# Four graph layers on one core: places of the adds computed ahead of their waits, layer 1's scores and one-hots in another form, and the last layer's adds dealt out between linked operations

## The chip, the cores and the metric

One NeuronCore of a Trainium2 chip runs the whole kernel as a single program. The metric is the device time of one execution in microseconds (us); less is better.

## The reference

`x` holds 3125 nodes of 256 features; 53125 edges (25000 in both directions and 3125 loops), sorted by target, join them. Four layers follow each other. Each normalises `x`, adds a sum over the edges and a linear attention over all nodes ("mix"), and then a feed-forward part of eight experts. What matters here is the sum over the edges:

```
layer 0:  x += elu-like( sum over edges of weight * (xn @ W)[src] ) + mix0(xn)
layer 1:  score[e,h] = sum over d of q[dst,h,d] * (k[src,h,d] + relation[type,d])
          alpha = softmax of score over the edges of one target
          x += f( sum over edges of alpha * v[src] ) + mix1(xn)
layer 2:  like layer 1 with logits  leaky_relu(s[src] + t[dst]), 8 heads
layer 3:  x += relu( segment_sum( (xn @ W)[src] * edge_weight, dst ) )
             + x-mixing: K,Q = elu+1; KV = K^T V; out = Q KV / (Q sum K);
               layer_norm(out @ Wm); relu([x, out] @ W1) @ W2; layer_norm
```

## The kernel before, in words

The edges are packed into 440 **steps** of 128 edges each. All targets of a step lie in one tile of 125 nodes, and a register holds the tile's number. In every layer a step goes through the same stations: the rows of its 128 sources are fetched (GpSimd issues an indirect DMA in layers 0, 2 and 3 and in the scores of layer 1; in layer 1's sums SyncE loads rows that were kept in order), a **one-hot** matrix (edge by node of the tile) is made on VectorE by comparing a ramp 0..124 with each edge's local target, TensorE multiplies one-hot by rows into a PSUM bank (the pages show it as two MATMULs per step), and VectorE's **add** puts the bank onto the rows of `total` that belong to the step's tile. The next step may go to the same tile, so every add waits for the one ahead of it (semaphore `added`) as well as for its own product (`summed`). TensorE may run ahead of the adds by as many banks as there are: 7 in layers 0 and 1, 3 in layers 2 and 3. The place of the add in `total` depends on the tile's register, so VectorE's queue computes an address by a register operation. It stands in the order lists as `ISA` and in the trace as `DVEq FUSED_REGOPS`.

Nothing schedules this at run time: each engine's instructions stand in the order in which the Python functions emit them, and semaphores tie the engines together.

- **Layer 0**, `Sums` (`gathered_sums`): per step one one-hot with its weight (`match`, eight steps ahead, L854) and one add (L880).
- **Layer 1, scores**, `edge_scores`: two steps form a **pair**. In a **turn** VectorE adds the relation (L3249), multiplies with the query the pair of the turn before (L3253), and sums over the 64 features of each head the pair of two turns before (L3257) if its number is even; odd pairs are summed on ScalarE, by eight activations with an accumulator (L3171). Only then are the pair's 2 of 12 row slots free for the next fetch of 256 KB. Layer 1's mixing (`MemoryMix`: `pe_turn`, `act_turn`, `dve_turn`) is cut into turns as well and rides along; ScalarE's share of a turn stands behind the scores of that turn.
- **Layer 1, sums**, `weighted_sums`: GpSimd multiplies the rows with alpha (L3438), the one-hots are made for eight steps at a time (`compare`, L3458), the add is L3466, and 24 slots hold rows.
- **Layer 2**, `Attend`: adds in L3977, each eighth in L3979, amid ten other operations on VectorE.
- **Layer 3**, `WeighedSums` in `gnn3_mix3`: one-hots for eight steps (L919), weights on ScalarE (L912), adds in L943. The mixing stands in **slots** (`kv`, `context`, then for thirteen node runs `q`, `read0`, `read1`, `out`, `turn`, `hidden`, `y`). A slot has steps in proportion to its work: 11 in `hidden`, 5 or 6 in `y`, 3 in `out`, 1 or 2 in the reads. TensorE does a slot's mixing first and then its steps. VectorE does the slot's adds first and then its mixing, except in `read0` and `read1`. Much of that mixing is a chain of small operations, each waiting for the one before (`link`).

Of the kernel before, what the change touches and what calls it, by code (L numbers as in the profile page):

```python
# [8 lines left out]
ALU = mybir.AluOpType  # L9
# [6 lines left out]
D = 256  # L16
P = 125
# [41 lines left out]
class Chain:  # L59
# [16 lines left out]
    def link(self, ins):  # L76
        self(ins)
        self.settle()

# [732 lines left out]
class Sums:  # L812
# [69 lines left out]

class WeighedSums(Sums):
# [48 lines left out]
    def add(self, v, s):  # L932
# [6 lines left out]
        tile = self.tiles.at(s)  # L939
        v.wait_ge(self.summed, s + 1)  # L940
        v.wait_ge(self.added, s)
        there = self.total[:, bass.ds(tile, 1), :]
# [1676 lines left out]
def gnn3_mix3(core):  # L2619
# [10 lines left out]
    with Phase(nc, "g3") as outer:  # L2630
        gnn3_front(core, table)
        total = outer.sb("total", [P, NT, D])
        with Phase(nc, "m3") as ph:
# [149 lines left out]
            def _(v):  # L2783
                link = Chain(v, mixing.chain_sem).link
# [28 lines left out]
                v.wait_ge(mixing.loaded, mixing.nload)  # L2813
                for (stage, r, _), steps in zip(slots, spans):
                    if stage not in ("read0", "read1"):
                        for s in steps:
                            sums.add(v, s)
# [6 lines left out]
                    elif stage == "read0":  # L2824
                        mixing.read_dve(v, link, r, 0)
                        for s in steps:
                            sums.add(v, s)
                        if r >= 2:
                            normalise(r - 2)
                    elif stage == "read1":  # L2830
                        mixing.read_dve(v, link, r, 1)
                        for s in steps:
                            sums.add(v, s)
# [8 lines left out]
                    elif stage == "y":  # L2842
# [14 lines left out]
class MemoryMix:  # L2857
# [107 lines left out]
    def act_turn(self, act, turn):  # L2965
        nc, H = self.core.nc, self.H
        if turn == self.LENGTHS + NODE_LOOPS - 1:
            act.wait_ge(self.summed, 1)
            nc.scalar.activation(self.root[:], self.total[:], ACT.Sqrt).then_inc(self.rooted, 1)
        if turn == self.SHIFT + 9:  # L2970
            act.wait_ge(self.kshift, 1)
            nc.scalar.activation(self.memk[:], self.memk[:], ACT.Exp).then_inc(self.mem_grown, 1)
        t = turn - self.CONTEXT
        if 0 <= t < NT:
# [5 lines left out]
        o, j = divmod(turn - self.READ, self.PERIOD)  # L2980
        if 1 <= o <= NODE_LOOPS and j == 0:
            act.wait_ge(self.summed2, o)
            nc.scalar.activation(self.root2[:], self.total2[:], ACT.Sqrt).then_inc(self.rooted2, 1)
        if 0 <= o < NODE_LOOPS:
            if j == BODY + 3:
                act.wait_ge(self.qshift, o + 1)
                nc.scalar.activation(self.q, self.q, ACT.Exp).then_inc(self.qgrown, 1)
            k, stage = divmod(j - 12, 2)
            if 0 <= k < BODY:
                t = o * BODY + k  # L2990
                if stage == 0:
                    act.wait_ge(self.turned, t + 1)
                    if t >= 2:
                        act.wait_ge(self.read, t - 1)
                    nc.scalar.activation(self.qT[:, t % 2, :], self.banks[t % 2][:, 0:P], ACT.Copy).then_inc(self.qkept, 1)
                else:
                    act.wait_ge(self.read, t + 1)
                    if t >= 2:
                        act.wait_ge(self.result, t - 1)
                    nc.scalar.activation(self.outT[:, t % 2, :], self.banks[t % 2][:, 128:128 + P], ACT.Copy).then_inc(self.okept, 1)  # L3000
# [104 lines left out]
def edge_scores(core, name, table, kept, query, relation, factor, scores, heads):  # L3105
# [11 lines left out]

    def pair_on_act(pair):
        return pair % 2 == 1

    def pairs_of_act(pair):
        return sum(pair_on_act(p) for p in range(pair + 1))

    with Phase(nc, name) as ph:
# [8 lines left out]
        expanded, shifted, multiplied, scored, act_scored = (ph.sem(n) for n in ("expanded", "shifted", "multiplied", "scored", "act_scored"))  # L3133
# [42 lines left out]
        @block.gpsimd  # L3176
        def _(pool):
            for s in range(STEPS):
                k = s % SLOTS
                if s >= SLOTS:  # L3180
                    pair = (s - SLOTS) // 2
                    if pair_on_act(pair):
                        pool.wait_ge(act_scored, pairs_of_act(pair))
                    else:
                        pool.wait_ge(scored, pair + 1 - pairs_of_act(pair))
# [30 lines left out]
        def _(v):  # L3216
# [24 lines left out]
            for turn in range(PAIRS + 2):  # L3241
# [12 lines left out]
                if 2 <= turn and not pair_on_act(turn - 2):  # L3254
# [5 lines left out]
            v.wait_ge(scored, PAIRS - pairs_of_act(PAIRS - 1))  # L3260
            v.wait_ge(act_scored, pairs_of_act(PAIRS - 1))
# [130 lines left out]
def weighted_sums(core, name, source, alpha, heads, total, own, values):  # L3392
# [5 lines left out]
    SLOTS, BANKS = 24, 7  # L3398
    PAIRS = STEPS // 2
    dim = D // heads  # L3400
    with Phase(nc, name) as ph:
        rows = ph.sb("rows", [W, SLOTS, D + heads])
        same = ph.sb("same", [W, 3, GROUP, P])
# [37 lines left out]
        def _(pe):  # L3441
            for s in range(STEPS):
# [3 lines left out]
                if s % GROUP == 0:  # L3446
                    pe.wait_ge(same_set, s // GROUP + 1)
                if s >= BANKS:
                    pe.wait_ge(added, s - BANKS + 1)
                nc.tensor.matmul(banks[s % BANKS][0:P, 0:D + heads], same[:, s // GROUP % 3, s % GROUP, :], rows[:, s % SLOTS, :], start=True, stop=True).then_inc(summed, 1)  # L3450

        @block.vector
        def _(v):
            def compare(g):
                shape = [W, GROUP, P]
                if g >= 3:
                    v.wait_ge(summed, GROUP * (g - 2))
                nc.vector.tensor_tensor(same[:, g % 3], bcast_mid(ramp[:, 0:P], shape), bcast_last(core.local[:, g * GROUP:(g + 1) * GROUP], shape),  # L3458
                                        ALU.is_equal).then_inc(same_set, 1)

            def add(s):
                tile = tiles.at(s)
                v.wait_ge(summed, s + 1)
                v.wait_ge(added, s)
                there = total[:, bass.ds(tile, 1), :]
# [8 lines left out]
            compare(0)  # L3474
            compare(1)
# [301 lines left out]
class Attend:  # L3777
# [190 lines left out]
    def add(self, v, s):  # L3968
# [3 lines left out]
        v.wait_ge(self.summed, s + 1)  # L3972
        if s:
            v.wait_ge(self.added, s)
        there, bank = self.total[:, bass.ds(tile, 1), :], self.banks[s % self.BANKS][0:P, 0:D + self.heads].unsqueeze(1)
# [338 lines left out]
```

## Time and profile before

| | |
|---|---|
| times of 3 runs | 6445.46, 6431.71, 6440.05 us |
| median | 6440.05 us |
| the profiled execution's own time | 6485.74 us |
| its span, first to last instruction | 6484.0 us |
| TensorE busy | 4404.0 us (68%) |
| VectorE busy | 3177.3 us (49%) |
| ScalarE busy | 1424.5 us (22%) |
| GpSimd busy | 2731.1 us (42%) |
| mean granted TensorE clock | 0.799 of full speed |

The kernel is a row of phases with barriers between them, so the shares of the whole say little: each phase has an engine, a queue or a chain of its own that sets its length. Line numbers are those of the kernel before.

### The profile page before, as it was taken

To read this page: it belongs to the slowest core of one execution; us is meant where nothing else is said; L and a number is where in the kernel's file an instruction comes from. 1 tells how busy PE (TensorE), PEld (TensorE's weight loads), DVE (VectorE), ACT (ScalarE), POOL (GpSimd) and SP (SyncE) were. 2 spreads that over 40 slices of the span, in tenths; PEclk is the share of its full clock that TensorE was granted. 3 is DMA by queue.
4 is the path that set the end of the run, shared out by engine and by line. 5 is a ranking of instruction groups with operands and counts; after the bars stand their busy time and mean duration, and the time that the engine had idled before them with its cause. 6 is when DMAs were issued, how large, how long until landed. Compare 5 with 4: busy or idle time off the path is not lost. (4 is left out here: it accounts for less than half of the span.)

```text
span 6484.0 us, 70548 instructions
## 1 busy us (share of the span) xinstructions
PE 4404.0 (68%) x18134; PEld 3067.0 (47%) x18134; DVE 3177.3 (49%) x7287; ACT 1424.5 (22%) x4712; POOL 2731.1 (42%) x2772
## 2 busy tenths in 40 slices
PE   0398855556795666664883946878759996788743
PEld 0256533334583343332342834666537774566543
DVE  7235444443004556666773135788842224577622
ACT  0022200002222233331132311100023333333211
POOL 1456656661101545553663035666400005566332
PEclk9988866667898575556995977887779998899776
DMA  4100023333012778884633224433310003222323
GB/s 150 53 2 2 2 66 92 92 91 88 34 35 85 235 231 236 241 235 143 187 94 107 72 70 106 106 102 103 69 40 0 0 2 100 77 87 88 77 97 107
DMA packets 407853, 616.81 MB, mean 95 GB/s; under 512 B 76553, under 2 KB 304286, under 8 KB 407109
## 3 DMA queue, kind: packets, MB, share of 16 engines
q0 software_dynamic: 124448, 324.61, 18.3%
q1 hardware_dynamic: 279908, 284.99, 13.9%
q10 hardware_dynamic: 3154, 3.20, 0.2%
q8 instruction: 147, 2.41, 0.2%
q14 instruction: 196, 1.60, 0.1%
HBM read 475.70 MB, written 137.50 MB: 95 GB/s over the span
## 5 line engine op out<-in xcount | busy, mean ns | idle before, releaser
L838 POOL DMA_INDIRECT m_rows<-support,far_at x440 | 444.3, 1010 | 989.9 <-POOLq L97 746.5
L3187 POOL DMA_INDIRECT g_sc_rows<-keyval,src_at x440 | 431.6, 981 | 492.7 <-DVE g1b_scores L3257 275.5
L3813 POOL DMA_INDIRECT g_sp_rows<-h,src_at x440 | 456.3, 1037 | 276.5 <-PE g_sp_bank L3862 142.8
L848 PE MATMUL g_sums_bank<-g_sums_rows,g_sums_same 128*125 128x256 f32 x880 | 351.8, 539 | 294.7 <-issue 277.4
L493 POOL DMA_INDIRECT records<-record,place_at x416 | 419.0, 1007 | 282.5 <-issue 121.0
L838 POOL DMA_INDIRECT g_sums_rows<-h,far_at x440 | 415.9, 945 | 232.2 <-issue 116.0
L3206 PE MATMUL g_sc_pair<-g1q_parts,g_sc_near 125*128 x1320 | 330.1, 381 | 151.6 <-DVE g_sc_rows L3253 100.5
L848 PEld LDWEIGHTS g_sums_bank<-g_sums_rows,g_sums_same 128*125 128x125 f32 x880 | 200.9, 257 | 445.6 <-issue 398.3
L3862 PE MATMUL g_sp_bank<-g_sp_rows,g_sp_same 128*125 128x264 f32 x880 | 315.1, 467 | 117.3 <-DVE g_total L3977 61.6
L880 DVE TENSOR_TENSOR g_total<-g_total,g_sums_bank 125x256 f32 x440 | 182.7, 415 | 336.2 <-issue 150.0
L906 PE MATMUL m_half<-m_rows,m_marks 128*125 128x256 f32 x880 | 268.8, 425 | 106.2 <-issue 76.4
L3171 ACT ACTIVATE g_sc_rows<-g_sc_rows 128x64 f32<-128x64 f32 x880 | 211.9, 242 | 518.7 <-DVE g_sc_rows L3253 415.6
L3450 PE MATMUL g_sp_bank<-g_sp_rows,g_sp_same 128*125 128x260 f32 x880 | 280.9, 427 | 53.9 <-DVE g_total L3466 36.3
L943 DVE TENSOR_TENSOR g_total<-g_total,m_half 125x256 f32 x440 | 184.6, 420 | 241.8 <-PE m_half L906 109.7
L3438 POOL TENSOR_TENSOR g_sp_rows<-g_sp_rows,g_alpha 128x512 f32<-128x512 f32 x220 | 226.7, 1042 | 173.4 <-DMA g_sp_rows<-kept 171.9
L3249 DVE TENSOR_TENSOR g_sc_rows<-g_sc_rows,g_sc_pair 128x512 f32<-128x512 f32 x220 | 150.2, 683 | 285.1 <-DMA f_back<-answer_rows,f_place_at 120.0
L1378 DVE SCALAR_TENSOR_TENSOR x<-f_y,f_comb,x 125x256 f32 x200 | 96.7, 483 | 376.4 <-PE f_y L1195 376.4
L1672 POOL DMA_INDIRECT f_back<-answer_rows,f_place_at x100 | 95.1, 951 | 411.4 <-DMA answer_rows<-f_answer 381.6
L1237 ACT ACTIVATE f_hid<-f_h,f_shift,f_scale 128x375 f32<-128x375 f32 (+1 forms) x320 | 195.4, 611 | 286.4 <-PE f_h L1174 280.6
L906 PEld LDWEIGHTS m_half<-m_rows,m_marks 128*125 128x125 f32 x880 | 160.6, 202 | 191.8 <-issue 119.8
L3862 PEld LDWEIGHTS g_sp_bank<-g_sp_rows,g_sp_same 128*125 128x125 f32 x880 | 165.1, 216 | 178.5 <-issue 101.8
L3206 PEld LDWEIGHTS g_sc_pair<-g1q_parts,g_sc_near 125*128 125x128 bf16 x1320 | 137.3, 119 | 217.5 <-issue 169.2
(702 smaller groups left out, 9995.7 us busy)
## 6 DMA issues: line engine op xcount, KB each, us to landing
kept<-g_sc_rows SPq DMA_DIRECT2D x440, 128.0 KB
g_sp_rows<-kept SPq DMA_DIRECT2D x440, 128.0 KB
xnT<-sorted_rows SPq DMA_DIRECT2D x80, 256.0 KB
answer_rows<-f_answer SPq DMA_DIRECT2D x64, 256.0 KB
g_sc_local_in<-local_rows SPq DMA_DIRECT2D x55, 250.0 KB
g_sp_local_in<-local_rows SPq DMA_DIRECT2D x55, 250.0 KB
answer_rows<-zero SPq DMA_DIRECT2D x1, 9856.0 KB
sorted_rows<-zero SPq DMA_DIRECT2D x1, 8192.0 KB
```

The source lines that it names most:

```text
L493: nc.gpsimd.indirect_dma_start(core.records, bass.IndirectOffsetOnAxis(ap=core.place_at[:, t:t + 1], axis=0), core.record[:, t, :], None). ...
L838: nc.gpsimd.indirect_dma_start(self.rows[:, k, :], None, self.table, bass.IndirectOffsetOnAxis(ap=core.far_at[:, s:s + 1], axis=0)).then_i ...
L848: nc.tensor.matmul(self.halves[s % slots], self.same[:, s % self.RING, :], self.rows[:, s % self.SLOTS, :], start=True, stop=True).then_in ...
L906: nc.tensor.matmul(self.halves[s % slots], self.mark(s), self.rows[:, s % self.SLOTS, :], start=True, stop=True).then_inc(self.summed, 1)
L1237: nc.scalar.activation(hid[layer][:, i % 2, mo, 0:n], hbank[q % HR][:, 0:n], func, scale=scale[layer][:, g, mo:mo + 1], bias=shift[layer][ ...
L3171: ins = nc.scalar.activation(product, product, ACT.Copy, accum_out=scores[:, h, s:s + 1])
L3187: nc.gpsimd.indirect_dma_start(rows[:, k, :], None, table, bass.IndirectOffsetOnAxis(ap=core.src_at[:, s:s + 1], axis=0)).then_inc(gathere ...
L3206: nc.tensor.matmul(banks[pair % PAIR_BANKS][:, s % 2, 0:D], near[:, g % 2, k * W:(k + 1) * W], query[:, i, bass.ds(tile, 1), :].rearrange( ...
L3438: nc.gpsimd.tensor_tensor(mine, mine, alpha[:, 2 * pair:2 * pair + 2, :].unsqueeze(3).to_broadcast([W, 2, heads, dim]), ALU.mult).then_inc ...
L3450: nc.tensor.matmul(banks[s % BANKS][0:P, 0:D + heads], same[:, s // GROUP % 3, s % GROUP, :], rows[:, s % SLOTS, :], start=True, stop=True ...
L3813: nc.gpsimd.indirect_dma_start(self.rows[:, k, :], None, self.table, bass.IndirectOffsetOnAxis(ap=core.src_at[:, s:s + 1], axis=0)).then_i ...
L3862: nc.tensor.matmul(self.banks[s % self.BANKS][0:P, 0:D + self.heads], self.same[:, g % 2, k, :], self.rows[:, s % self.SLOTS, :], start=Tr ...
```

## The change

Four edits, in the words of the code:

1. Every `add` (four classes or functions) lowers its place (`v.lower_ap(there)`), that is emits the register operation, ahead of its two waits, and waits for `added` before `summed`.
2. `edge_scores`: all pairs are summed on VectorE; ScalarE's program is layer 1's mixing alone, written out in order (`act_program`).
3. `weighted_sums`: a one-hot is made per step, eight steps ahead, in a ring of 16, in place of one instruction for eight steps.
4. `gnn3_mix3`: `Woven` holds back up to a number of a slot's adds (`links`) and emits one behind each linked operation of the slot's mixing; what is left follows at its end.

```diff
+class Woven(Chain):
+    def __init__(self, eng, sem, fill):
+        Chain.__init__(self, eng, sem)
+        self.fill, self.left = fill, []
+    def open(self, steps, ahead):
+        self.left = list(steps)
+        while len(self.left) > ahead:
+            self.next()
+    def next(self):
+        if self.left:
+            self.fill(self.eng, self.left.pop(0))
+    def close(self):
+        while self.left:
+            self.next()
+    def link(self, ins):
+        self(ins)
+        count = self.n
+        self.next()
+        self.settle(count)
...
         tile = self.tiles.at(s)
+        there = self.total[:, bass.ds(tile, 1), :]
+        v.lower_ap(there)
+        v.wait_ge(self.added, s)
         v.wait_ge(self.summed, s + 1)
-        v.wait_ge(self.added, s)
-        there = self.total[:, bass.ds(tile, 1), :]
...
-                link = Chain(v, mixing.chain_sem).link
+                woven = Woven(v, mixing.chain_sem, sums.add)
+                link = woven.link
...
+                links = {"kv": 0, "context": 0, "q": 0, "read0": 6, "read1": 2, "out": 7, "turn": 0, "hidden": 8, "y": 7}
                 for (stage, r, _), steps in zip(slots, spans):
-                    if stage not in ("read0", "read1"):
-                        for s in steps:
-                            sums.add(v, s)
+                    woven.open(steps, links[stage])
...
                     elif stage == "read0":
                         mixing.read_dve(v, link, r, 0)
-                        for s in steps:
-                            sums.add(v, s)
...
+                    woven.close()
...
-            for turn in range(PAIRS + 1):
-                if turn and pair_on_act(turn - 1):
-                    act.wait_ge(multiplied, turn)
-                    for s in (2 * turn - 2, 2 * turn - 1):
-                        for h in range(heads):
-                            product = rows[:, s % SLOTS, h * dim:(h + 1) * dim]
-                            ins = nc.scalar.activation(product, product, ACT.Copy, accum_out=scores[:, h, s:s + 1])
-                    ins.then_inc(act_scored, 1)
-                if turn < PAIRS:
-                    mix.act_turn(act, turn)
+            mix.act_program(act)
...
-                if 2 <= turn and not pair_on_act(turn - 2):
+                if 2 <= turn:
...
-            def compare(g):
-                shape = [W, GROUP, P]
-                if g >= 3:
-                    v.wait_ge(summed, GROUP * (g - 2))
-                nc.vector.tensor_tensor(same[:, g % 3], bcast_mid(ramp[:, 0:P], shape), bcast_last(core.local[:, g * GROUP:(g + 1) * GROUP], shape),
-                                        ALU.is_equal).then_inc(same_set, 1)
+            def compare(s):
+                if s >= RING:
+                    v.wait_ge(summed, s - RING + 1)
+                nc.vector.tensor_scalar(same[:, s % RING, :], ramp[:, 0:P], core.local[:, s:s + 1], None, ALU.is_equal).then_inc(same_set, 1)
...
             for s in range(STEPS):
+                if s + AHEAD < STEPS:
+                    compare(s + AHEAD)
                 add(s)
-                if s % GROUP == 1 and s // GROUP + 2 < GROUPS:
-                    compare(s // GROUP + 2)
```

VectorE's order in layer 1's sums. A semaphore number is shared by phases and shows under its first name: here `m0_hid_made` is `summed` and `m0_hid_kept` is `added`; `g_sp_bank` is the product, and `TENSOR_LOAD` fetches eight tile numbers. Before, at the end of a group of eight steps:

```order
L3466 ISA [waits m0_hid_kept,m0_hid_made]
L3466 TENSOR_TENSOR g_total<-g_total,g_sp_bank 125x260
L3458 TENSOR_TENSOR g_sp_same<-g_sp_ramp,local 128x1000 [waits m0_hid_made]
L3466 ISA [waits m0_hid_kept,m0_hid_made]
L3466 TENSOR_TENSOR g_total<-g_total,g_sp_bank 125x260
L806 TENSOR_LOAD step_tile
L3466 ISA [waits m0_hid_kept,m0_hid_made]
```

With the change, in the same stretch:

```order
L3461 TENSOR_TENSOR g_total<-g_total,g_sp_bank 125x260 [waits m0_hid_made,m0_hid_kept]
L835 TENSOR_LOAD step_tile
L3453 TENSOR_SCALAR g_sp_same<-g_sp_ramp,local 128x125 [waits m0_hid_made]
L838 ISA
L3461 TENSOR_TENSOR g_total<-g_total,g_sp_bank 125x260 [waits m0_hid_made,m0_hid_kept]
L3453 TENSOR_SCALAR g_sp_same<-g_sp_ramp,local 128x125 [waits m0_hid_made]
```

The waits moved from the register operation (`ISA`) to the add, and a one-hot of 125 columns stands between any two adds.

VectorE in a `hidden` slot of layer 3. `m_n_stat`, `m_ytile` and `x` are the chain that ends a node run, `m_half` the products, `m_marks` the one-hots of eight steps. Before, behind the slot's eleven adds:

```order
L943 ISA [waits m0_turn_kept,m0_turned]
L943 TENSOR_TENSOR g_total<-g_total,m_half 125x256
L2051 TENSOR_TENSOR m_n_stat<-m_n_stat 125x2 [waits g1_sc_m_shifted]
L2052 TENSOR_TENSOR m_n_stat<-m_n_stat 125x2 [waits g1_sc_m_kturned]
L2053 TENSOR_SCALAR m_n_stat<-m_n_stat 125x2 [waits g1_sc_m_kturned]
L2054 TENSOR_TENSOR m_n_stat<-m_n_stat 125x2 [waits g1_sc_m_kturned]
```

With the change, in the same place of the program:

```order
L2082 TENSOR_TENSOR m_n_stat<-m_n_stat 125x2 [waits g1_sc_m_v_kept]
L949 TENSOR_TENSOR m_marks<-ramp,near_local 128x1000 [waits m0_turned]
L838 ISA
L974 TENSOR_TENSOR g_total<-g_total,m_half 125x256 [waits m0_turned,m0_turn_kept]
L2083 TENSOR_TENSOR m_n_stat<-m_n_stat 125x2 [waits g1_sc_m_diag_set]
L838 ISA
L974 TENSOR_TENSOR g_total<-g_total,m_half 125x256 [waits m0_turned,m0_turn_kept]
L2084 TENSOR_SCALAR m_n_stat<-m_n_stat 125x2 [waits g1_sc_m_diag_set]
```

Eight of the eleven adds now stand one by one behind the links of that chain; three stand ahead of it.

VectorE in the scores. Before, a turn with a sum, a turn without one, and the turn after it:

```order
L3257 TENSOR_REDUCE g1b_scores<-g_sc_rows 128x2x4 [waits f0_back_in2]
L3249 TENSOR_TENSOR g_sc_rows<-g_sc_rows,g_sc_pair 128x2x256 [waits m0_finished,ends_turned_done,ends_tiled]
L3253 TENSOR_TENSOR g_sc_rows<-g_sc_rows,g_sc_pair 128x2x256 [waits m0_attention_in]
L3249 TENSOR_TENSOR g_sc_rows<-g_sc_rows,g_sc_pair 128x2x256 [waits m0_finished,ends_saved,ends_kept]
L3253 TENSOR_TENSOR g_sc_rows<-g_sc_rows,g_sc_pair 128x2x256 [waits m0_attention_in]
L3257 TENSOR_REDUCE g1b_scores<-g_sc_rows 128x2x4 [waits f0_back_in2]
```

With the change:

```order
L3255 TENSOR_REDUCE g1b_scores<-g_sc_rows 128x2x4 [waits f0_back_in2]
L3247 TENSOR_TENSOR g_sc_rows<-g_sc_rows,g_sc_pair 128x2x256 [waits m0_finished,ends_turned_done,ends_tiled]
L3251 TENSOR_TENSOR g_sc_rows<-g_sc_rows,g_sc_pair 128x2x256 [waits m0_attention_in]
L3255 TENSOR_REDUCE g1b_scores<-g_sc_rows 128x2x4 [waits f0_back_in2]
L3247 TENSOR_TENSOR g_sc_rows<-g_sc_rows,g_sc_pair 128x2x256 [waits m0_finished,ends_saved,ends_kept]
```

Every turn now has its sum, 110 more in all.

## Rows read from the trace of the kernel before

**Rows 1.** Windows; engines' busy us, instructions, granted clock, DMA share, GB/s.

```profile
876.00:1514.00 638.00, 349.42 (x876) 199.00 (x874) 301.58 (x872) 0.00 (x0) 408.75 (x433) 0.65 0.32 90
2112.00:2935.00 823.00, 544.65 (x3121) 302.62 (x3121) 502.63 (x882) 263.90 (x1882) 420.48 (x429) 0.61 0.79 234
3014.00:3342.00 328.00, 280.88 (x880) 131.68 (x880) 242.78 (x494) 43.37 (x208) 223.24 (x217) 0.99 0.61 183
3985.00:4690.00 705.00, 576.99 (x2323) 435.37 (x2322) 566.20 (x1318) 67.66 (x208) 425.39 (x408) 0.82 0.38 97
5410.00:5562.00 152.00, 110.55 (x351) 66.39 (x350) 55.90 (x120) 49.16 (x159) 102.24 (x105) 0.91 0.30 90
5562.00:6107.00 545.00, 433.74 (x1703) 323.32 (x1702) 379.21 (x939) 189.28 (x496) 327.64 (x329) 0.90 0.29 80
```

The columns after the length are TensorE, its weight loads, VectorE, ScalarE, GpSimd. The stretches are layer 0's sums, layer 1's scores, layer 1's sums, layer 2's sums, and layer 3's sums while `kv` runs and after it.

**Rows 2.** Timeline of VectorE, layer 1's sums; start, duration, [idle before].

```profile
3149.47 1.19 DVE L3458 TENSOR_TENSOR g_sp_same<-g_sp_ramp,local 128x1000 f32<-128x1000 f32 x1
3150.58 0.41 DVE L3466 TENSOR_TENSOR g_total<-g_total,g_sp_bank 125x260 f32 x1
3151.21 0.42 DVE L3466 TENSOR_TENSOR g_total<-g_total,g_sp_bank 125x260 f32 x1 [0.21 <-DVE g_total L3466]
...
3155.36 1.19 DVE L3458 TENSOR_TENSOR g_sp_same<-g_sp_ramp,local 128x1000 f32<-128x1000 f32 x1
```

**Rows 3.** Line L3466; duration min/median/max in ns, first and last start.

```profile
L3466 DVEq FUSED_REGOPS  x440: 57/57/65, 3017.0 to 3342.0; - x147
L3466 DVE TENSOR_TENSOR g_total<-g_total,g_sp_bank x440: 412/425/427, 3017.1 to 3342.1; 125x260 f32 x147
```

**Rows 4.** Groups by line, layer 1's sums on GpSimd.

```profile
L3438 POOL TENSOR_TENSOR g_sp_rows<-g_sp_rows,g_alpha 128x512 f32<-128x512 f32 x220 | 226.7, 1042 | 173.4 <-DMA g_sp_rows<-kept 171.9
```

**Rows 5.** Groups by line and form on VectorE: nearest to the new one-hot.

```profile
L3087 DVE TENSOR_SCALAR g_sc_msquare<-g_sc_mbank,g_sc_minverse 125x128 f32<-125x128 f32 x25 | 8.5, 341 | 0.0
L854 DVE TENSOR_SCALAR g_sums_same<-g_sums_ramp,near_local,near_weight 128x125 f32<-128x125 f32 x440 | 176.1, 402 | 0.1
```

**Rows 6.** Timeline of VectorE, layer 0's sums.

```profile
1099.59 0.41 DVE L880 TENSOR_TENSOR g_total<-g_total,g_sums_bank 125x256 f32 x1
1099.92 0.40 DVE L854 TENSOR_SCALAR g_sums_same<-g_sums_ramp,near_local,near_weight 128x125 f32<-128x125 f32 x1
1100.24 0.41 DVE L880 TENSOR_TENSOR g_total<-g_total,g_sums_bank 125x256 f32 x1
```

**Rows 7.** Lines L880 and L943, the adds of layers 0 and 3.

```profile
L880 DVE TENSOR_TENSOR g_total<-g_total,g_sums_bank x440: 405/415/423, 876.0 to 1513.4; 125x256 f32 x147
...
L943 DVE TENSOR_TENSOR g_total<-g_total,m_half x440: 406/421/423, 5412.1 to 6106.8; 125x256 f32 x147
```

**Rows 8.** Timeline, layer 3, a `hidden` slot's end: VectorE.

```profile
5824.71 0.15 DVE L2051 TENSOR_TENSOR m_n_stat<-m_n_stat 125x2 f32<-125x2 f32 x1
...
5828.06 0.69 DVE L2807 TENSOR_TENSOR m_ytile<-m_ytile,m_beta 125x512 f32<-125x512 f32 x1
...
5832.49 0.42 DVE L943 TENSOR_TENSOR g_total<-g_total,m_half 125x256 f32 x1 [0.49 <-issue]
```

**Rows 9.** The same stretch: TensorE.

```profile
5825.63 1.89 PE L2009 MATMUL m_ctx<-m_wout,m_outT 128*125 128x256 f32 x8
5833.01 1.61 PE L906 MATMUL m_half<-m_rows,m_marks 128*125 128x256 f32 x3 [5.49 <-issue]
```

**Rows 10.** Groups by line, VectorE in layer 2: every eighth add.

```profile
L3979 DVE SCALAR_TENSOR_TENSOR g_total<-g_total,g_sp_ratio,g_sp_bank 125x264 f32 x55 | 26.8, 488 | 21.2 <-PE g_sp_bank L3862 13.2 <-DVE g_total L3977 4.9 <-issue 2.3
```

**Rows 11.** Groups by line, layer 1's scores: sums on VectorE.

```profile
L3257 DVE TENSOR_REDUCE g1b_scores<-g_sc_rows 128x8 f32<-128x512 f32 x110 | 74.6, 678 | 0.0
```

**Rows 12.** Groups by line, layer 1's scores: sums on ScalarE.

```profile
L3171 ACT ACTIVATE g_sc_rows<-g_sc_rows 128x64 f32<-128x64 f32 x880 | 211.9, 242 | 518.7 <-DVE g_sc_rows L3253 415.6 <-issue 103.0
L3171 ACT ACTIVATION_READ_ACCUMULATOR g_sc_rows<-g_sc_rows 128x1 f32 x880 | 164.2, 187 | 0.0
```

**Rows 13.** Waits in 2112 to 2933: total us, times, longest.

```profile
PE g_sc_mbank L2963 <- ACT g_sc_mqT L2995: 58.7, 23, 4.8
```

More of the change, by code:

```diff
@@ L939, in add @@
         tile = self.tiles.at(s)
+        there = self.total[:, bass.ds(tile, 1), :]
+        v.lower_ap(there)
+        v.wait_ge(self.added, s)
         v.wait_ge(self.summed, s + 1)
-        v.wait_ge(self.added, s)
-        there = self.total[:, bass.ds(tile, 1), :]
         nc.vector.tensor_tensor(there, there, self.halves[s % len(self.halves)].unsqueeze(1), ALU.add).then_inc(self.added, 1)
@@ L2831, in _ @@
                         mixing.read_dve(v, link, r, 1)
-                        for s in steps:
-                            sums.add(v, s)
                     elif stage == "out":
@@ L2963, in pe_turn, with act_program @@
                 nc.tensor.matmul(self.banks[t % 2][:, 128:128 + P], self.context[:], self.qT[:, t % 2, :], start=True, stop=True).then_inc(self.read, 1)
-    def act_turn(self, act, turn):
+    def act_program(self, act):
         nc, H = self.core.nc, self.H
[L2967 to L2974, printed above, removed]
+        act.wait_ge(self.summed, 1)
+        nc.scalar.activation(self.root[:], self.total[:], ACT.Sqrt).then_inc(self.rooted, 1)
+        act.wait_ge(self.kshift, 1)
+        nc.scalar.activation(self.memk[:], self.memk[:], ACT.Exp).then_inc(self.mem_grown, 1)
+        for t in range(NT):
             act.wait_ge(self.shifted, t + 1)
@@ L2979, in act_turn @@
             nc.scalar.activation(self.kv[:, t % 2, 0:H], self.kv[:, t % 2, 0:H], ACT.Exp).then_inc(self.kgrown, 1)
-        o, j = divmod(turn - self.READ, self.PERIOD)
-        if 1 <= o <= NODE_LOOPS and j == 0:
-            act.wait_ge(self.summed2, o)
-            nc.scalar.activation(self.root2[:], self.total2[:], ACT.Sqrt).then_inc(self.rooted2, 1)
[L2984 to L3000, printed above, removed]
+        for o in range(NODE_LOOPS):
+            act.wait_ge(self.qshift, o + 1)
+            nc.scalar.activation(self.q, self.q, ACT.Exp).then_inc(self.qgrown, 1)
+            for t in range(o * BODY, (o + 1) * BODY):
+                act.wait_ge(self.turned, t + 1)
+                if t >= 2:
+                    act.wait_ge(self.read, t - 1)
+                nc.scalar.activation(self.qT[:, t % 2, :], self.banks[t % 2][:, 0:P], ACT.Copy).then_inc(self.qkept, 1)
+                act.wait_ge(self.read, t + 1)
+                if t >= 2:
+                    act.wait_ge(self.result, t - 1)
+                nc.scalar.activation(self.outT[:, t % 2, :], self.banks[t % 2][:, 128:128 + P], ACT.Copy).then_inc(self.okept, 1)
+            act.wait_ge(self.summed2, o + 1)
+            nc.scalar.activation(self.root2[:], self.total2[:], ACT.Sqrt).then_inc(self.rooted2, 1)
     def dve_begin(self, v):
@@ L3116, in edge_scores @@
     dim = D // heads
[L3118 to L3122, printed above, removed]
     with Phase(nc, name) as ph:
@@ L3180, in _ @@
                 if s >= SLOTS:
[L3181 to L3185, printed above, removed]
+                    pool.wait_ge(scored, (s - SLOTS) // 2 + 1)
                     pool.wait_ge(stashed[k], 16 * (s // SLOTS))
@@ L3397, in weighted_sums @@
     nc = core.nc
-    SLOTS, BANKS = 24, 7
+    SLOTS, BANKS, RING, AHEAD = 24, 7, 16, 8
     PAIRS = STEPS // 2
@@ L3402, in weighted_sums @@
         rows = ph.sb("rows", [W, SLOTS, D + heads])
-        same = ph.sb("same", [W, 3, GROUP, P])
+        same = ph.sb("same", [W, RING, P])
         loaded = [ph.sem(f"loaded{k}") for k in range(SLOTS)]
@@ L3473, in _ @@
             tiles.load(0)
-            compare(0)
-            compare(1)
+            for s in range(AHEAD):
+                compare(s)
             for s in range(STEPS):
+                if s + AHEAD < STEPS:
+                    compare(s + AHEAD)
                 add(s)
-                if s % GROUP == 1 and s // GROUP + 2 < GROUPS:
-                    compare(s // GROUP + 2)
                 if s % GROUP == 2 and s // GROUP + 1 < GROUPS:
@@ L3971, in add @@
         tile = self.tiles.at(s)
-        v.wait_ge(self.summed, s + 1)
+        there = self.total[:, bass.ds(tile, 1), :]
+        v.lower_ap(there)
         if s:
             v.wait_ge(self.added, s)
-        there, bank = self.total[:, bass.ds(tile, 1), :], self.banks[s % self.BANKS][0:P, 0:D + self.heads].unsqueeze(1)
+        v.wait_ge(self.summed, s + 1)
+        bank = self.banks[s % self.BANKS][0:P, 0:D + self.heads].unsqueeze(1)
         if k:
```

15 lines of the change are left out of this document (7 added, 8 removed).

## The prediction, made before the changed kernel ran

> **What bounds the kernel now.** Barriers stand between the phases, so I read the windows of each phase first [rows 1], then lines and timeline inside it, to see which wait ends last there.
>
> Layer 0's sums last 638 us with TensorE busy for 349 us at a clock of 0.65 and VectorE for 302 us. The adds run from 876.0 to 1513.4 [rows 7], 637.4 us or 1.45 us a step, while in a stretch of ready work an add follows the last one after 1100.24 − 1099.59 = 0.65 us with a one-hot between them [rows 6]. So neither engine sets the pace; the rows' arrival does. Layer 3's `kv` part issues 105 gathers in 152 us, 1.45 us each again [rows 1]: the same bound.
>
> Layer 1's sums are another thing. 440 adds lie between 3017.1 and 3342.1, 0.74 us a step [rows 3]. Eight steps take 3155.36 − 3149.47 = 5.89 us [rows 2]: seven intervals of 0.63 us from add to add (0.425 of work, 0.21 idle, of which the register operation is 57 ns [rows 3]) and a one-hot of 1.11 us from its start to the next add's. VectorE never rests for anything but its own last add. TensorE's clock is 0.99, and the transfers are at 183 GB/s where the scores reach 234 [rows 1].
>
> Layer 1's scores last 823 us at a DMA share of 0.79, the highest in the kernel, with no engine above 545 us [rows 1]: 3.74 us for each of 220 pairs, mostly the fetch into the slots.
>
> In layer 3 behind `kv`, 545 us, TensorE is busy for 434 us, VectorE for 379 us [rows 1]. At a `hidden` slot's end VectorE runs the chain from 5824.71 to 5832.49 without an add [rows 8], and TensorE, with its three banks full, stands still for 5.49 us before its next step [rows 9].
>
> **The change part by part.** The sum is made against the profiled execution's 6485.74 us (1.7 us above its span), which lies 0.7% above the median of 6440.05.
>
> *Places ahead of waits.* Where a one-hot stands between adds, the register operation already ran in the queue under it, so layer 0 gets nothing; even if it got 57 ns a step, the adds wait for the gather there. Bounds 0 and, for lack of any row that speaks for more, 0.
>
> *Layer 1's sums.* Per step now one one-hot and one add. The nearest row to a one-hot of 125 columns with one pointer operand is 341 ns at 128 columns; the same compare with a second operand takes 402 [rows 5]. Successive operations overlap by 0.085 us, as between 1099.59 + 0.41 and 1099.92 [rows 6]. So 0.341 − 0.085 = 0.256 for the one-hot, and 0.425 − 0.085 = 0.34 for the add: 0.596 us a step, 440 × 0.596 = 262 us for 325, **−63 us**. The semaphore of the last add has 0.256 us to arrive where the idle row shows 0.21 needed, so it should be covered, only just. With layer 0's measured 0.65 it is 286 us, −39; the good end is −66 (the one-hot at 0.25). Other floors: GpSimd's multiplication takes 1042 ns for two steps [rows 4], 0.52 a step; the loads at 234 GB/s would need 328 × 183/234 = 257 us. Both lie just under 262, so they are what is late next, and a reason why nothing beyond −66 can come.
>
> Against this speaks that 440 operations take the place of 55. If the one-hots came on top, with the adds' idle time untouched, they would cost 440 × 0.256 − 55 × 1.11 = 113 − 61 = +52 us. The rows of layer 0 bear on it: there a compare of 402 ns per step fits between adds at 0.65 in all, which on top of an idle time of 0.21 it could not. The Trainium skill, "VectorE: DVE Perf Modes", section "Rules for kernel authors", states a rule of the first kind: in chained operations it is their count that should be kept small, not the semaphores. By that rule the phase would lose the 52 us; the trace of layer 0 does not agree with it for this pair of operations.
>
> *Layer 1's scores.* VectorE gets 110 sums more, at 678 ns or 74.6 us in all [rows 11]. ScalarE loses 880 activations of 242 ns and their 880 reads of 187 [rows 12], 3.42 us per odd pair. VectorE goes from 503 to 577 of 823 us, so it has room; where its own turns are long, at the mixing's loops, it does not. In return the mixing's copies on ScalarE no longer queue behind scores: TensorE's wait for them is 58.7 us over 23 times [rows 13], most of which the fetch would fill again. Bounds +75 (nothing hidden) and −59; the fetch sets the pace in between, so I take **0**.
>
> *Layer 2.* Only each eighth add follows an add directly; its idle time is 21.2 us over 55 [rows 10], of which 13.2 is named as TensorE's. The register operation and a part of the semaphore go: **−5**, between 0 and −10.
>
> *Layer 3.* The adds run from 5412.1 to 6106.8 [rows 7], 694.7 us; at the gather's pace, layer 0's 637.4, is the floor, so at most −57. In `hidden`, eight adds of 0.63 us now fill the chain's gaps: each costs 0.34 to 0.42 there and starts while the link settles, so 8 × (0.63 − 0.38) = 2.0 us per slot, and for 13 slots 26 us on VectorE; `y`, `out` and `read0` hold 7, 7 and 6 and so all their few steps, but their adds mostly wait for TensorE. More is in TensorE's 5.49 us: with a bank freed every 0.7 us it keeps moving; 13 × 5.49 = 71 us would be the whole, above the floor of 57. The `kv` part (152 us) gives nothing. Between 0 and −57 I take **−25**, the VectorE sum, nearest to what is worked out from rows.
>
> Sum: −63 + 0 − 5 − 25 = −93: 6485.74 − 93 = 6393, times 6440.05/6485.74 gives **6347 us**.
>
> **Rivals.** 0.2% (13 us) is about what a measurement of this kernel can tell from no change.
>
> 1. *Layer 3 wins nothing*: the gather there is late whatever VectorE does, as `kv` shows. 6372. Chance 0.12. Against it: TensorE's idle time stands behind VectorE's chain, not behind a transfer [rows 9].
>
> 2. *The scores' sums are not hidden*: +75, 6422. The DMA share of 0.79 and 320 us of room speak against it, the turns at the mixing's loops for it. 0.13.
>
> 3. *A register operation ahead of its wait brings nothing and the step takes 0.65*: sums −39, layer 3 −10: 6391. 0.08.
>
> 4. *Held adds stall the chain (ends slower)*: an add between two links waits for its product, and the chain, the reads and TensorE's next slot stand behind it on VectorE's queue. If rows come at 1.45 us a step instead of the adds' 0.63, eight adds cost 8 × 0.82 = 6.6 us per `hidden` slot, 85 us in all: 6347 + 25 + 85 = 6457. It decides from (93 − 25)/13 = 5.2 us per slot on. TensorE standing idle for banks, not rows, speaks against it. 0.06.
>
> 5. *The scores suffer twice*: the sums in full, and odd pairs' slots released later. ScalarE had a pair after 3.42 us; VectorE has it a turn later, 3.74 + 0.68, so 1.0 us later for each loop of 12 slots (6 pairs), 37 us more. +112: 6459. 0.03.
>
> 6. *The one-hots come on top*: the adds' idle time stays and each one-hot adds 0.256, +52 in place of −63: 6347 + 115 = 6462. Layer 0's rows speak against it. 0.03. It is what the rule of "VectorE: DVE Perf Modes" in the Trainium skill would lead to.
>
> **How the numbers follow.** The forecast as worked out has 0.55 (own range 6320 to 6375: layer 1's sums at 0.65, layer 3 from −10 to −50). Cases 4 to 6 hold 0.12, and 0.01 of case 2 lies above 6427; a bit over a third of this, where such a loss is smaller than worked out, falls within 6427 to 6453. So faster 0.87, same 0.05, slower 0.08. The range reaches down to 6290 (layer 3 at its floor of −57, −32 more than taken, and half of the −59 in the scores would be 6286) and up to 6425, which takes in cases 1 to 3 and leaves out 4 to 6.
>
> **What the changed profile would show.** In layer 1's sums: adds 0.60 us apart with a one-hot of some 0.34 between them, no idle time on VectorE, the line's first and last start 262 us apart, GpSimd's or the loads' waits shorter than a turn. If the adds stand 0.65 apart, case 3 holds; if idle time of 0.2 stands behind the one-hot, case 6 does. In the scores: 220 sums at 678 ns, the phase within 10 us of 823; ScalarE near 60 us busy. If it is longer, the idle time ahead of GpSimd's gather names VectorE's sum. In layer 3: eight adds between the links with no idle time ahead of them, TensorE's pause of 5.49 us gone, the adds 670 us from first to last. If the chain's adds show waits for `m_half`, case 4 holds. In layer 0 and `kv`: no change. What would make it wrong above all is layer 3, where gains and stalls hang on the same three banks, and the scores, where a long turn of VectorE is passed on to the fetch.

## The result, and the profile after

Whole runs: the median is 6349.98 us (4 runs, 6340.24 to 6361.85) beside 6441.88 us for the kernel before (4 runs, 6431.71 to 6445.46). The ratio is 0.9861, 95% interval 0.984 to 0.9881: 92 us faster. The profiled execution of after spans 6338.5 us.

The windows by phase, in the order and with the columns of [rows 1]:

```profile
877.00:1507.00 630.00, 419.31 (x876) 205.36 (x874) 310.67 (x872) 0.00 (x0) 408.56 (x433) 0.59 0.32 91
2108.00:2876.00 768.00, 539.19 (x3121) 296.60 (x3121) 563.47 (x992) 46.08 (x122) 426.02 (x428) 0.62 0.82 250
2954.00:3227.00 273.00, 262.83 (x880) 131.56 (x880) 265.62 (x881) 43.37 (x208) 221.75 (x217) 0.99 0.73 220
3861.00:4543.00 682.00, 561.44 (x2316) 428.90 (x2316) 563.13 (x1318) 67.47 (x208) 419.30 (x408) 0.83 0.39 100
5261.00:5413.00 152.00, 107.19 (x347) 65.52 (x347) 55.32 (x119) 47.54 (x155) 104.75 (x106) 0.92 0.30 91
5413.00:5962.00 549.00, 417.41 (x1708) 319.71 (x1706) 355.59 (x946) 192.44 (x501) 332.50 (x330) 0.91 0.29 80
```

Layer 1's sums went from 328 to 273 us, near the forecast. Two phases did not do as forecast: layer 1's scores went from 823 to 768 us, layer 3's last part from 545 to 549.

The timeline of VectorE in layer 1's sums, as in [rows 2]:

```profile
3100.04 0.41 DVE L3461 TENSOR_TENSOR g_total<-g_total,g_sp_bank 125x260 f32 x1
3100.37 0.34 DVE L3453 TENSOR_SCALAR g_sp_same<-g_sp_ramp,local 128x125 f32<-128x125 f32 x1
3100.63 0.41 DVE L3461 TENSOR_TENSOR g_total<-g_total,g_sp_bank 125x260 f32 x1
3100.96 0.34 DVE L3453 TENSOR_SCALAR g_sp_same<-g_sp_ramp,local 128x125 f32<-128x125 f32 x1
3101.22 0.41 DVE L3461 TENSOR_TENSOR g_total<-g_total,g_sp_bank 125x260 f32 x1
3101.73 0.35 DVE L3453 TENSOR_SCALAR g_sp_same<-g_sp_ramp,local 128x125 f32<-128x125 f32 x1
```

No idle time is left: an add follows an add after 0.59 us (3100.63 − 3100.04). Only in the third the next one-hot starts 0.51 us behind its add, not 0.33: the load of eight tile numbers stands between them.

The same stretch of program in layer 3 as in [rows 8], a `hidden` slot of after:

```profile
5708.27 1.33 DVE L974 TENSOR_TENSOR g_total<-g_total,m_half 125x256 f32 x3 [2.25 <-PE m_half L936]
5709.52 0.15 DVE L2082 TENSOR_TENSOR m_n_stat<-m_n_stat 125x2 f32<-125x2 f32 x1
5709.64 0.42 DVE L974 TENSOR_TENSOR g_total<-g_total,m_half 125x256 f32 x1
...
5717.54 0.41 DVE L974 TENSOR_TENSOR g_total<-g_total,m_half 125x256 f32 x1
5717.87 1.71 DVE L2028 RECIPROCAL m_inverse<-m_inverse 128x250 f32<-128x250 f32 x1
5719.61 0.42 DVE L2031 SCALAR_TENSOR_TENSOR m_outT<-m_nd,m_inverse 128x250 f32<-128x250 f32 x1
5719.95 0.86 DVE L974 TENSOR_TENSOR g_total<-g_total,m_half 125x256 f32 x2
```

The add fits in where the link before only settled: 5709.64 lies 0.12 us behind a link whose successor stood 0.19 us behind it before. From this first add to the next slot's it is 11.7 us (5708.27 to 5719.95) with 0.22 us of idle time, where the slot whose end [rows 8] show took 16.3 (5816.16 to 5832.49). Of the 4.6 us between them, 1.1 is a second one-hot for eight steps that fell into the stretch before only. TensorE's pause at the slot's end, 5.49 us in [rows 9], is down to 1.57:

```profile
5720.46 1.12 PE L936 MATMUL m_half<-m_rows,m_marks 128*125 128x256 f32 x4 [1.57 <-issue]
```

But the slot's first add now waits 2.25 us for TensorE, where it waited 0.94 before, and what is gained in the slot is lost elsewhere, in the groups by line over all of layer 3's adds (5412 to 6107 before, 5263 to 5962 after):

```profile
L943 DVE TENSOR_TENSOR g_total<-g_total,m_half 125x256 f32 x440 | 184.6, 420 | 241.8 <-PE m_half L906 109.7 <-DMA g_sp_rows<-h,src_at 54.3 <-issue 39.7
```

```profile
L974 DVE TENSOR_TENSOR g_total<-g_total,m_half 125x256 f32 x440 | 183.9, 418 | 226.3 <-PE m_half L936 107.9 <-DMA g_sp_rows<-h,src_at 86.7 <-issue 24.4
```

The idle time ended by a transfer (a gather, shown under its queue's first name) grew from 54.3 to 86.7 us, while the idle time ended by the last add fell from 37.6 to 2.3.

### The profile page after: what moved, and what is told of

Its sections match the earlier page's. It is cut to its first block and busy times, and to the rows that moved or that the text cites. A ratio compares the mean times of both kernels' runs of the same rounds, so it can differ in the third digit from the quotient of the medians.

```text
span 6338.5 us, 67901 instructions
## 1 busy us (share of the span) xinstructions
PE 4420.4 (70%) x18134; PEld 3057.7 (48%) x18134; DVE 3242.0 (51%) x7782; ACT 1208.3 (19%) x2952; POOL 2737.1 (43%) x2772
## 5 line engine op out<-in xcount | busy, mean ns | idle before, releaser
L877 PE MATMUL g_sums_bank<-g_sums_rows,g_sums_same 128*125 128x256 f32 x880 | 421.7, 604 | 218.2 <-issue 203.3
L936 PE MATMUL m_half<-m_rows,m_marks 128*125 128x256 f32 x880 | 255.0, 417 | 135.0 <-issue 70.4
L3446 PE MATMUL g_sp_bank<-g_sp_rows,g_sp_same 128*125 128x260 f32 x880 | 262.8, 419 | 17.0 <-DVE g_sp_same L3453 10.9
L3857 PEld LDWEIGHTS g_sp_bank<-g_sp_rows,g_sp_same 128*125 128x125 f32 x880 | 164.1, 214 | 165.4 <-issue 82.6
L3446 PEld LDWEIGHTS g_sp_bank<-g_sp_rows,g_sp_same 128*125 128x125 f32 x880 | 131.6, 187 | 148.2 <-issue 98.9
```

Source lines behind the costliest of these rows:

```text
L877: nc.tensor.matmul(self.halves[s % slots], self.same[:, s % self.RING, :], self.rows[:, s % self.SLOTS, :], start=True, stop=True).then_in ...
L936: nc.tensor.matmul(self.halves[s % slots], self.mark(s), self.rows[:, s % self.SLOTS, :], start=True, stop=True).then_inc(self.summed, 1)
L3857: nc.tensor.matmul(self.banks[s % self.BANKS][0:P, 0:D + self.heads], self.same[:, g % 2, k, :], self.rows[:, s % self.SLOTS, :], start=Tr ...
```

## The experiments

Each kernel was timed beside the kernel before on the same chip. Chip 13 ran a1 to a4, chip 0 ran b1 to b4, chip 12 ran c1 to c4; which one ran the first pair, before and after, is not known. They were of two kinds: where the kernel before takes 6437 to 6442 us, layer 0's adds last 628 to 637 us (before, after and c1 to c4); where it takes 6067 to 6077 us, they last 550 us (a1 to a4, b1 to b4). I speak of the slower and the faster chips. Lengths of phases come from one profiled execution of each kernel; layer 3's, unedited, differ by 8 us between a1 and a2 on one chip. The length of a phase is given from its first to its last add; for the scores from the first multiplication (L3253) to the last sum on VectorE.

### Each part alone (a faster chip)

**a1**: hunks of part 2 alone, on the kernel before. **a2**: part 3 and its `lower_ap` alone. **a3**: part 4 alone. **a4**: part 1 in layers 0, 2 and 3 alone. The edits are the hunks of the diff above.

> Only the scores' edit is made: all pairs summed on VectorE, ScalarE runs the mixing alone. Theory A (the trace with all four edits, in which the scores last from the first relation add at 2117.3 to the last sum at 2874.2, 757 us, against 2121.4 to 2934.7, 813 us): the edit is worth 40 to 56 us, so about 6395 us for 6442. Rival B (the forecast): the fetch sets the pace, the edit is worth 0, 6442 us, and the difference of the two traces was one execution's. Rival C: the sums are not hidden and it costs up to 75 us.

> Only layer 1's sums are edited: a one-hot per step, the place computed ahead of the waits in this phase. A and B alike: the adds go from 325 us to about 269 (first add to last, as in the trace with all edits), 0.61 us a step, so 6386 us for 6442. The forecast's own value was 262. A rival in which the profiled phase was lucky gives 286 (0.65 a step) and 6403.

> Only the last layer is edited: adds dealt out between the links; places stay behind the waits. Theory A (in the two traces the adds last 694.7 and 697.6 us): worth nothing, 6442 us, adds 690 to 700 us. Rival B (the forecast): minus 15 to 25 us, about 6420 us, adds about 672 us.

> Only the places of layers 0, 2 and 3 are lowered ahead of the waits. Theory A (traces: layer 2's adds 699.7 to 676.9 us, layer 0's 637.4 to 629.5): up to 23 us in layer 2 and 8 in layer 0, 6411 us. Rival B (the forecast): 5 us in layer 2, a few in layer 3, nothing in layer 0, 6435 us, the rest of the difference of the traces being that the execution profiled before was 0.7% above its median.

The kernel before took 6076.91 us (18 runs).

| | us | ratio (95%) | what its phase shows |
|---|---|---|---|
| a1 scores | 6069.95 | 0.9994 (0.9985 to 1.0003) | scores 668.7, unedited in a2 to a4 672.2 to 679.3 |
| a2 sums | 6014.19 | 0.9899 (0.9883 to 0.9914) | adds 269.9, unedited 324.8 to 325.5 |
| a3 dealt out | 6054.75 | 0.997 (0.996 to 0.9981) | layer 3 603.2, unedited in a1, a2 624.4, 616.5 |
| a4 places | 6036.78 | 0.9942 (0.9928 to 0.9955) | layer 3 594.9; layer 2 651.0, unedited 659.6 to 664.3 |

The scores' edit is worth nothing that can be told on this chip. Layer 3 gains from both edits, and the places, which I had given next to nothing there, gain the more. Layer 0 stays at 550 us in all four.

### All four, and all but one (a faster chip)

**b1** is the changed kernel, **b2** the kernel before, **b3** and **b4** leave out part 4 and part 2.

> The changed kernel itself, timed beside its parts. The four parts alone gave 1.0%, 0.66%, 0.3% and 0.06% (sum 2.05%) where the first four sets of whole runs gave 1.4% on a slower chip. Theory A: the parts add up except for layer 3, where places and dealing out draw on the same idle time: 0.980 to 0.983 where layer 0's adds take 550 us. Where they take about 637 us (slower arrival of rows), layer 3 is at the gather's floor and gives less: 0.986.

> The kernel before, for its profile on the chip of this batch. Theory A: layer 0's adds are at the same length as in the others of this batch, layer 1's sums 325 us, and layer 3's 617 to 625 us on a chip where layer 0 takes 550, 695 us where it takes 637.

> The changed kernel, but the last layer's adds are ahead of the mixing again, not dealt out. Theory A (both draw on the same idle time): layer 3's adds 595 us, 5 us or less slower than with all four. Rival B (the gains add): 17 to 22 us slower than with all four.

> The changed kernel, but odd pairs are summed on ScalarE again. Theory A (the fetch sets the pace of the scores on any chip): within 6 us of all four. Rival B (on a chip with slower arrival the earlier release is worth what the two first traces differ by): 40 to 56 us slower than all four, if this batch's chip is slow.

The kernel before took 6067.34 us (9 runs).

| | us | ratio (95%) | scores | L1 sums | layer 2 | layer 3 |
|---|---|---|---|---|---|---|
| b1 all four | 5955.99 | 0.9808 (0.9793 to 0.9823) | 672.8 | 269.1 | 647.1 | 580.4 |
| b2 before | 6070.58 | one run | 671.5 | 325.2 | 658.3 | 620.6 |
| b3 without dealing out | 5964.99 | 0.9828 (0.9813 to 0.9843) | 675.2 | 269.4 | 650.0 | 597.7 |
| b4 without scores | 5960.75 | 0.982 (0.9806 to 0.9833) | 680.0 | 269.3 | 647.5 | 576.6 |

Here the change is worth 1.9%, and the four parts alone, 1.95% by their ratios, add up to it. My theory that places and dealing out draw on the same idle time falls by the profiles: without dealing out layer 3 is 17 us longer, where it gained 13 to 21 us alone (603.2 for 616.5 and 624.4). By the whole runs the intervals of b1 and b3 overlap, so the 9 us between the medians alone would prove nothing. b4 is not told from b1. The lines of layer 3's adds in b2 and in b1:

```profile
L943 DVE TENSOR_TENSOR g_total<-g_total,m_half 125x256 f32 x440 | 184.8, 420 | 171.3 <-PE m_half L906 123.4 <-DVE g_total L943 44.6 <-issue 2.6
```

```profile
L974 DVE TENSOR_TENSOR g_total<-g_total,m_half 125x256 f32 x440 | 183.4, 417 | 136.1 <-PE m_half L936 123.9 <-DVE g_total L974 5.4 <-issue 1.5
```

On this chip no add waits for a transfer in either, and what went is the wait for the last add, 44.6 to 5.4 us. These 39 us are about what the phase lost, 40.

### What the place and the one-hot are worth apart (a slower chip)

**c1**, on the changed kernel:

```diff
-                there = total[:, bass.ds(tile, 1), :]
-                v.lower_ap(there)
-                v.wait_ge(added, s)
                 v.wait_ge(summed, s + 1)
+                v.wait_ge(added, s)
+                there = total[:, bass.ds(tile, 1), :]
```

**c2** is the same edit the other way round (place ahead, then the waits for `added` and `summed`) in `weighted_sums` of the kernel before, whose one-hots stay eight at a time. In both, the order of the two waits turns together with the place, as it does in the change; no run parts the two.

> The changed kernel, but in layer 1's sums the register operation stands behind its waits again; the one-hots stay one per step. Theory A: the one-hot alone hides the add's 0.21 us; the place costs nothing behind it: adds 269 to 272 us from first to last, as with all four. Rival B: the register operation and its wait for the last add come behind the one-hot: an add follows an add after 0.65 us (as in layer 0 before), 286 us plus the eighth-step loads, about 295.

> The kernel before, but in layer 1's sums the register operation stands ahead of its waits, with the one-hots for eight steps at a time. Theory A: the 57 ns operation leaves the gap and nothing more: 7 intervals of 0.63 become 0.57, 440 x 7/8 x 0.06 = 23 us less, 302 us of adds. Rival B: the gap of 0.21 is the semaphore's alone: no change, 325 us. Rival C: the wait behind the operation is cheaper too: gap 0.1, about 285 us.

The kernel before took 6436.64 us (7 runs) in this call. c1: 6382.99 us, ratio 0.9913 (0.989 to 0.9935). c2: 6367.82 us, ratio 0.9895 (0.9875 to 0.9915), 69 us less. The changed kernel was not timed in this call. The lines of the adds, c1 and then c2:

```profile
L3460 DVE TENSOR_TENSOR g_total<-g_total,g_sp_bank x440: 414/426/427, 2965.9 to 3264.6; 125x260 f32 x147
```

```profile
L3467 DVE TENSOR_TENSOR g_total<-g_total,g_sp_bank x440: 412/424/427, 2997.3 to 3252.7; 125x260 f32 x147
```

298.7 us with the one-hots per step and the place behind, 255.4 with the place ahead and the one-hots in eights, 269.1 with both edits. Neither theory for c2 went far enough. Its timeline on VectorE:

```profile
3149.43 3.62 DVE L3467 TENSOR_TENSOR g_total<-g_total,g_sp_bank 125x260 f32 x8
3152.97 1.19 DVE L3458 TENSOR_TENSOR g_sp_same<-g_sp_ramp,local 128x1000 f32<-128x1000 f32 x1
3154.08 2.25 DVE L3467 TENSOR_TENSOR g_total<-g_total,g_sp_bank 125x260 f32 x5
```

Eight adds in 3.62 us without a gap, although each waits for the one ahead: 0.45 us from add to add where it was 0.63, and 4.65 us for eight steps (3154.08 − 3149.43) where it was 5.89. The one-hots in eights cost 1.11 us per group; one per step costs 8 × 0.26.

The records of VectorE's queue show what filled the gap. In the kernel before, where an add follows an add directly (386 times, medians), the last add's end is followed by 39 ns until the record of the wait for `added`, which takes 21, 48 ns until the register operation, which takes 57, and 47 ns until the next add: 0.21 us one behind the other. In c2 the wait that stands by itself is the one for `summed`; it and the register operation run while the last add does, the wait for `added` is on the add itself, and the add starts 34 ns behind the last one's end. With the place ahead but the wait for `added` still by itself, 39 + 21 + 48 = 0.11 us of the gap would be left; that is an estimate from these records. By it, 0.10 of the 0.18 us gained are the register operation's and 0.07 the order of the waits.

In c1 the timeline shows what a one-hot alone does:

```profile
3099.97 0.43 DVE L3460 TENSOR_TENSOR g_total<-g_total,g_sp_bank 125x260 f32 x1
3100.31 0.34 DVE L3453 TENSOR_SCALAR g_sp_same<-g_sp_ramp,local 128x125 f32<-128x125 f32 x1
3100.61 0.43 DVE L3460 TENSOR_TENSOR g_total<-g_total,g_sp_bank 125x260 f32 x1
```

0.64 us from add to add, rival B's step: no gain over 0.63, except that the group's 1.11 us is gone. The same 0.21 us lie between an add's end and the next add; the one-hot runs under them.

### More adds held, fewer slots in the scores (a slower chip)

```diff
-links = {... "hidden": 8, "y": 7}
+links = {... "hidden": 11, "y": 7}
```

```diff
-    SLOTS, PAIR_BANKS = 12, 3
+    SLOTS, PAIR_BANKS = 10, 3
```

> The changed kernel, with all eleven adds of a hidden slot held back, in place of eight. Theory A: the adds are cheap between the links, so three more of them save up to 13 x 3 x 0.2 = 8 us of layer 3. Rival B: the three held longer keep TensorE's three banks full while it could start, so layer 3 gets longer by some 13 x 1 us.

> The changed kernel, with 10 row slots in the scores in place of 12. Theory A (the loop through the slots sets the pace of the scores: a slot is fetched again only when its pair is summed): the scores go from 673 us towards 12/10 of it, 740 to 800 us. Rival B (GpSimd's issue or the transfer rate sets it): 673 to 690 us.

c3: 6354.55 us, ratio 0.9873 (0.9856 to 0.9891), not told from the change's 0.9861. Its layer 3 lasts 719.4 us where after, c1 and c4 have 697.6, 703.8 and 706.6: in the profile it is 13 to 22 us longer, as rival B had it; whether by its banks isn't shown. c4: 6392.9 us, ratio 0.9932 (0.9909 to 0.9955), slower than all four; its scores last 799.8 us where after, c1 and c3 have 755.7 to 761.2. That is 39 to 44 us or 5 to 6% more for a sixth fewer slots. The loop through the slots bounds the phase in part; the scores would be a fifth longer if it did all through.

## Why the prediction was right, and where it was not

The forecast was 92 to 93 us, and 92 were measured; but the terms met their sum partly by luck. Unedited phases on the slower chips are those of the kernel before and of c2, edited ones those of after, c1, c3 and c4, except where these change the phase themselves.

| term | forecast | slower chips, unedited | edited | a faster chip (b2 to b1) |
|---|---|---|---|---|
| layer 0 | 0 | 637.4, 633.4 | 628.5 to 629.8 | 549.8 to 550.3 |
| scores | 0 | 810.1, 797.1 | 755.7 to 761.2 | 671.5 to 672.8 |
| layer 1's sums | −63 | 325.0 | 269.1 to 269.6 | 325.2 to 269.1 |
| layer 2 | −5 | 699.7, 685.9 | 673.5 to 682.1 | 658.3 to 647.1 |
| layer 3 | −25 | 694.7, 690.2 | 697.6 to 706.6 | 620.6 to 580.4 |

**What bounds the kernel**: right for layer 1's sums. There the profile names TensorE's product, and not the last add, for most of the idle time before adds:

```profile
  PE g_sp_bank L3450: 70.2, 319
  DVE g_total L3466: 14.7, 68
```

But in c2, with TensorE's program unchanged, 1.9 us of it are left, so TensorE was not what held the adds. "Nothing beyond −66 can come" was wrong: GpSimd's 0.52 us a step make 229 us and are not just under 262, and c2 reached −70 with its loads at 230 GB/s. For layer 0 both kinds of chip show that the adds are not the bound: 550 us before and after on the faster, and 4 to 9 us less, of no clear cause, on the slower. For layer 3 it depends on the chip.

**Places ahead of waits** is the step that failed. I took them for hidden or for 57 ns. The idle 0.21 us of [rows 2] I gave to the semaphore, which "has 0.256 us to arrive where the idle row shows 0.21 needed". c2 shows that it needs almost none of it: adds that wait for each other run 0.45 us apart once the register operation doesn't stand behind the wait. The gap is a row of queue steps behind the last add (the wait's own record, the register operation and the time between them), of which the 57 ns are a part. How much the order of the waits has in it, which the edit turns too, is known only from the estimate above. This edit alone carries the gain of layer 1's sums (−70 us by c2's profile, −69 by its whole runs), and 22 to 30 us of layer 3 on a faster chip (a4's 594.9 for 616.5 to 624.4).

**Layer 1's sums**: −56 for −63. The working per step held to the digit: one-hot 342 ns for 341, 0.59 us a step for 0.596. Left out was the load of tile numbers, 0.18 us for each group of eight, 55 × 0.18 = 10 us. And the one-hots per step, which I took for the cause of the gain, cost 269.1 − 255.4 = 14 us in the presence of the places. Some 10 of the 14 are that load: it takes 0.59 to 0.62 us, and in c2 it runs under the one-hot of 1.19 us. The operations themselves are nearly even, 8 × 0.59 = 4.72 us for 4.65. Rival 6's mechanism did not come (no idle time stands behind the one-hots), but its direction did. The rule of the Trainium skill, "VectorE: DVE Perf Modes", section "Rules for kernel authors", to keep the count of chained operations small, agrees with c2 against after, by 14 us, of which 10 are the load, and not by the 52 that I worked out for it. Its other half, that it is not the semaphores, does not agree with c2 against the kernel before: as many VectorE operations, another order of waits and register operation, 70 us. Layer 0's row at 0.65 us per step, by which I set the rule aside, was read rightly: with the place ahead, in after, the steps are as long, so there the add and the one-hot of 402 ns fill them:

```profile
1081.37 0.41 DVE L910 TENSOR_TENSOR g_total<-g_total,g_sums_bank 125x256 f32 x1
1081.69 0.41 DVE L883 TENSOR_SCALAR g_sums_same<-g_sums_ramp,near_local,near_weight 128x125 f32<-128x125 f32 x1
1082.01 0.42 DVE L910 TENSOR_TENSOR g_total<-g_total,g_sums_bank 125x256 f32 x1
```

**Scores**: nothing on the faster chips (a1, b4), as forecast. On the slower, unedited 797 to 810, edited 756 to 761: 36 to 54 us less, though the edit alone was not timed there. The waits there answer to [rows 13]; in after:

```profile
PE g_sc_mbank L2991 <- ACT g_sc_mqT L3012: 2.8, 4, 1.3
```

58.7 us of waiting for ScalarE's copies are down to 2.8. I had this as the bound of −59 and chose 0, since the fetch would fill it again. It seems to where the DMA share is 0.90 (b2's scores, where this wait of 26.7 us went without a gain), not where it is 0.79. The fall of this wait and the gain go together on the slower chips, but no run parted it from the other thing that the edit does, the release of odd pairs' slots by VectorE. Against the latter speak the waits of GpSimd, which issues the fetches, in before and in after:

```profile
POOL g_sc_rows L3187 <- DVE g1b_scores L3257: 275.5, 78, 13.1
POOL g_sc_rows L3187 <- ACT g_sc_rows L3171: 0.3, 1, 0.3
POOL g_sc_rows L3185 <- DVE g1b_scores L3255: 217.7, 92, 15.7
```

ScalarE released its slots late only once, for 0.3 us, so that had next to nothing to give. What fell, by about the gain, is the wait for VectorE's sums: 275.5 and 264.2 us unedited (before, c2), 214.0 to 221.7 edited. That VectorE's turns got shorter through the copies is argued and not shown.

**Layer 3**: a gain of 40 us on a faster chip, none on the slower (3 to 16 us longer there). Rival 1's mechanism fits the slower chips: the rows came late, and the adds' idle time ended by a transfer rose from 54.3 and 59.8 us (before, c2) to 74.9 to 86.7 (after, c1, c4), where the faster chip has none. c3, at 61.9 us, doesn't fit it: its layer 3 is the longest all the same. So layer 3 was a term of −25 that came as about +10, and the scores a term of 0 that came as about −40; their errors cancelled.

**Layer 2**: −11 on a faster chip (a4 too: 651.0 for 660), −4 to −26 on the slower, for −5.

A version with the places ahead in all layers, the scores and the dealing out, but the one-hots in eights, should by these profiles be 14 us faster than the changed kernel, an estimate of 6336 us. It wasn't timed.

## What to carry to other kernels

Where an operation's address hangs on a register, have it computed ahead of the operation's waits, and wait for the operation before it first, so that this wait is on the operation itself: the two together took the gap between chained adds from 0.21 us to 0.03, though the register operation is 57 ns long. Look for such a gap between operations that "wait for each other" before filling it with other work; filling it costs what the filling costs. A phase's bound should be named with how near the next one is: here the same change gained 40 us or nothing in one phase, and nothing or 36 to 54 us in another, on chips where gathered rows arrived fast or slowly.

## What the runs showed of the hardware that was not expected

Chips differ by 6% in this kernel, and not evenly. Layer 0's 440 adds take 628 to 637 us or 550 us, the scores move 234 or 282 GB/s, while layer 1's sums last 325.0 and 325.2 us. On a faster chip GpSimd's gather issue (946 ns and on average 0.30 us idle, 1.25 us a step) is layer 0's pace. GpSimd in groups by line, the kernel before on a slower chip and then b2:

```profile
L838 POOL DMA_INDIRECT g_sums_rows<-h,far_at x432 | 408.3, 945 | 212.4 <-issue 113.9 <-remote 53.1 <-PE g_sums_bank L848 45.5
```

```profile
L838 POOL DMA_INDIRECT g_sums_rows<-h,far_at x433 | 409.4, 946 | 131.9 <-issue 99.3 <-PE g_sums_bank L848 32.6
```

The issues last as long on both, and the idle time between them is 80 us more on the slower. The median from issue to issue is 1.25 us on both; on the slower some gaps are longer, and 53.1 us of them end as "remote". So of the 1.45 us a step that the prediction put down to the rows' arrival alone, 1.25 are the pace of the issues.
